# A perceiver block on one core: where the second quad's stacks stand, the first chunk in slices, a bias negated later and ternary weights stored in halves

## The reference

```
q = split_heads(layernorm(x) @ Wq, 16) * 32 ** -0.5
k = split_heads(ctx @ Wk, 16);  v = split_heads(ctx @ Wv, 16)
logits = einsum('bhqd,bhkd->bhqk', q, k) + bias          # bias 128 x 2048, the same for all heads
x = x + merge_heads(softmax(logits) @ v) @ Wo
ws = 1.0 / clip(mean(abs(w)), 1e-5)                      # for each matrix w_i, w_f, w_g, w_o, w_gate, w_down
wq = clip(round(w * ws), -1, 1) / ws                     # the ternary weights
```

## Time and profile before

| | before |
|---|---|
| median of 3 runs | 1146.83 us |
| profiled execution | 1147.05 us, span 1145.3 us |
| attention (0 to 710 us) | TensorE busy 660.66 us |
| the rest (710 to 1145 us) | TensorE busy 353.41 us |
| whole span | TensorE 1014.1 us (89%), VectorE 578.0 (50%), ScalarE 429.7 (38%), GpSimd 237.4 (21%) |

### The profile page before, as it was taken

The page is one execution under the profiler, slowest core; times in us unless marked ns, Lnnn a source line. Parts: engine busy times, 40 slices in busy tenths (PEclk is TensorE's granted clock), DMA queues, the critical chain, the costliest instruction groups (busy, mean ns, idle before and its releaser), DMA issues.

```text
span 1145.3 us, 17470 instructions
## 1 busy us (share of the span) xinstructions
PE 1014.1 (89%) x7046; PEld 791.6 (69%) x7046; DVE 578.0 (50%) x1180; ACT 429.7 (38%) x552; POOL 237.4 (21%) x201
## 2 busy tenths in 40 slices
PE   5799899999899997899999998426659999999997
PEld 4478677888677885677887674223347999977774
DVE  4433886456894644794448873786752111111110
ACT  1111676152783182784234771545611011111110
POOL 0300560002630002620003900543111011110000
PEclk9899999999999998999999999667767999999999
DMA  7063781515754217554125818000018997699910
GB/s 267 27 112 81 166 197 43 187 37 150 156 142 169 112 37 210 127 138 137 44 97 119 175 35 346 17 0 1 1 45 306 389 374 274 214 359 313 296 19 12
DMA packets 77753, 169.85 MB, mean 148 GB/s; under 512 B 7416, under 2 KB 17656, under 8 KB 72800
## 3 DMA queue, kind: packets, MB, share of 16 engines
q1 hardware_dynamic: 75552, 163.84, 46.9%
q0 software_dynamic: 2112, 4.80, 1.9%
HBM read 118.97 MB, written 16.10 MB: 118 GB/s over the span
## 4 chain that ended last, share of the span: by engine, by line
PE 77%; DVE 9%; issue 4%; DMA 3%; ACT 3%; POOL 3%; SPq 0%; DVEq 0%; POOLq 0%; ACTq 0%
PE psum L1590 10%; PE psum L451 8%; PE psum L431 6%; PE psum L1620 6%; PE psum L466 6%; PE psum L1605 5%; PE psum L370 5%; PE psum L387 5%; PE psum L371 5%; PE psum L388 4%; PE psum L389 4%; PE psum L372 4%; PE psum L419 1%; DMA stack<-stack 1%; PE psum L492 1%
## 5 line engine op out<-in xcount | busy, mean ns | idle before, releaser
L849 POOL CAST stack<-kT 128x2048 fp32r<-128x2048 f32 x40 | 77.5, 1963 | 444.4 <-ACT kT L732 403.2
L603 DVE CUSTOM_DVE_ANT_0 prob<-psum,biasmap,top 128x512 f32<-128x512 f32 x192 | 144.2, 751 | 25.6 <-PE psum L431 17.2
L451 PE MATMUL psum<-ident,prob 128*128 128x128 f32 x1024 | 136.2, 276 | 5.9 <-ACT probT L778 3.9
L770 ACT ACTIVATE prob<-prob,top 128x2048 f32<-128x2048 f32 x64 | 128.6, 2009 | 24.2 <-DVE top L603 24.2
L451 PEld LDWEIGHTS psum<-ident,prob 128*128 128x128 f32 x1024 | 118.4, 142 | 24.6 <-issue 10.8
L1590 PE MATMUL psum<-xT,wring 128*128 128x128 f32 (+3 forms) x1024 | 133.5, 291 | 0.6 <-ACT xT L1878 0.6
L1590 PEld LDWEIGHTS psum<-xT,wring 128*128 128x128 f32 x1024 | 131.4, 193 | 2.8 <-issue 1.9
L778 ACT COPY probT<-psum 128x1024 f32<-128x1024 f32 x96 | 96.5, 1010 | 57.8 <-PE psum L466 56.5
L732 ACT COPY kT<-psum 128x512 f32<-128x512 f32 x64 | 37.5, 586 | 206.2 <-PE psum L372 206.2
L370 PE MATMUL psum<-ctx_part,wk_hi 128*128 128x512 f32 x256 | 101.7, 397 | 13.6 <-DVE ctx_part L541 13.6
L1801 DVE TENSOR_SCALAR hidden<-psum,b 128x128 f32<-128x128 f32 (+3 forms) x64 | 23.6, 369 | 161.9 <-PE psum L1590 161.9
(11 more groups left out here) (231 smaller groups left out, 1471.0 us busy)
## 6 DMA issues: line engine op xcount, KB each, us to landing
wring<-in_w SPq DMA_DIRECT2D x64, 1024.0 KB, 9.9
ctx_raw<-in_ctx_t SPq DMA_DIRECT2D x16, 1024.0 KB, 6.2
stack<-stack SPq DMA_DIRECT2D x40, 256.0 KB, 4.9
stack<-key_stack SPq DMA_DIRECT2D x28, 256.0 KB, 4.5
ternary<-ternary_weights SPq DMA_DIRECT2D x1, 6272.0 KB, 24.6
prob<-in_w_gate_t SPq DMA_DIRECT2D x1, 5632.0 KB, 17.2
query_stacks<-prob SPq DMA_DIRECT2D x16, 256.0 KB, 5.4
qstack<-query_stacks SPq DMA_DIRECT2D x16, 256.0 KB, 5.5
```

What stands on the lines that cost most here:

```text
L451: mm = pe.transpose(psum[:, w + i, j * P:(j + 1) * P], prob[:, prob_slot(n, j), kt * P:(kt + 1) * P], ident[:, :])
L603: dve.tensor_tensor_reduce(prob[:, slot, keys], psum[:, scores.of[n, j, c], :], biasmap[:, keys], 1.0, top[:, h, (c + 1) % 2:(c + 1) % 2 + ...
L770: act.activation(prob[:, slot, :], prob[:, slot, :], ACT.Exp, bias=top[:, h, 1:2], scale=-1.0, accum_out=top[:, h, 2:3]).then_inc(*raised. ...
```

## The change

There are five edits.

- **Stacks.** Heads 1 to 3 of the second quad leave the ring. Their stacks stand in the four slots of `prob` in which the first quad had its stacks, which are the slots that the second quad's own scores go to: head j's cast waits until head j of the first quad has been scored. Head 0 of the second quad keeps a place of the ring (turn 0), and the third and fourth quads have turns 1 to 8.
- **Fillers.** The 16 row blocks are spread as 2, 1, 2, 1, ... over ten slots, where they were 2, 2, 1, ... over nine.
- **Ternary weights.** The mean is taken one tile earlier, and the store is two DMAs of half the pieces, each issued when its half is ready. What waited for the store waits for the second half.
- **First chunk.** Wk and chunk 0 come in four pairs of DMAs, one pair for each row block k of 128 rows (256 KB each). ScalarE casts the two slices of a block, VectorE subtracts, and TensorE does the 12 matmuls of that block for all four key tiles before the next block.
- **Bias.** GpSimd waits for the last of the four normalised rows of x before it negates the bias.

```diff
-FILLERS = (2, 2, 1, 2, 2, 1, 2, 2, 2)
+FILLERS = (2, 1, 2, 1, 2, 1, 2, 1, 2, 2)
...
-        self.mean_at = self.sum_at + len(self.sums) + 3
+        self.mean_at = self.sum_at + len(self.sums) + 2
         self.round_at = self.mean_at + 1
-        self.store_at = self.round_at + len(self.pieces) + 1
+        self.stores = [(half, self.round_at + (half + 1) * len(self.pieces) // 2 + 1) for half in range(2)]
...
+        def in_ring(n, j):
+            return n % DT >= 2 or n % DT == 1 and j == 0
+
         def ring_turn(n, j):
-            return QUAD * (n % DT - 1) + j
+            return QUAD * (n % DT - 2) + j + 1 if n % DT >= 2 else 0
+
+        def head_of_turn(b, turn):
+            return (DT * b + 2 + (turn - 1) // QUAD, (turn - 1) % QUAD) if turn else (DT * b + 1, 0)
...
         def stack_place(n, j):
-            if n % DT == 0:
-                return early_stack[:, (QUAD * (n + 1) + j) % PS, :]
-            return RING_PLACES[ring_turn(n, j) % len(RING_PLACES)]
+            if in_ring(n, j):
+                return RING_PLACES[ring_turn(n, j) % len(RING_PLACES)]
+            return early_stack[:, (QUAD * (n - n % DT + 1) + j) % PS, :]
...
+            def project_first_keys():
+                banks = [work.take(("keys", 0, 0, m), keys_copied.at(0, 0, m))[0] for m in range(DT)]
+                for k in range(DT):
+                    pe.wait_ge(*slice_low.at(k, "ctx"))
+                    ch, cl = ctx_part[:, 0, 0, k, :], ctx_part[:, 0, 1, k, :]
+                    for m, w in enumerate(banks):
+                        wh, wl = wk_hi[:, k, m * P:(m + 1) * P], wk_lo[:, k, m * P:(m + 1) * P]
+                        pe.matmul(psum[:, w, :], wh, ch, start=(k == 0), stop=False)
+                        pe.matmul(psum[:, w, :], wh, cl, start=False, stop=False)
+                        mm = pe.matmul(psum[:, w, :], wl, ch, start=False, stop=(k == DT - 1))
+                        if k == DT - 1:
+                            mm.then_inc(*keys_projected.made(0, 0, m))
+
+            project_first_keys()
...
                         project_value_tile(b, VTILES * c + i)
-                    elif b == 0 or (c, i) > (0, 0):
+                    elif c > 0 or b > 0 and i > 0:
...
+                    dve.wait_ge(*ternary_stored.at(b, 1))
+                elif (g, j, c) == (1, 0, 0):
...
-            dve.wait_ge(*wk_in.at("all"))
-            split(wk_hi[:, :, :], wk_lo[:, :, :], wk_sb).then_inc(*parts_split.made("wk"))
-            split_chunk(0)
+            for k in range(DT):
+                dve.wait_ge(*slice_high.at(k, "wk"))
+                dve.tensor_tensor(wk_lo[:, k, :], wk_sb[:, k, :], wk_hi[:, k, :].bitcast(F32),
+                                  ALU.subtract).then_inc(*slice_low.made(k, "wk"))
+                dve.wait_ge(*slice_high.at(k, "ctx"))
+                dve.tensor_tensor(ctx_part[:, 0, 1, k, :], ctx_raw[:, k, :], ctx_part[:, 0, 0, k, :].bitcast(F32),
+                                  ALU.subtract).then_inc(*slice_low.made(k, "ctx"))
             dve.wait_ge(*wv_in.at("all"))
             split(wv_hi[:, :, :], wv_lo[:, :, :], wv_sb).then_inc(*parts_split.made("wv"))
...
+            for k in range(DT):
+                act.wait_ge(*slice_in[k].at("ctx"))
+                act.copy(wk_hi[:, k, :], wk_sb[:, k, :]).then_inc(*slice_high.made(k, "wk"))
+                act.copy(ctx_part[:, 0, 0, k, :], ctx_raw[:, k, :]).then_inc(*slice_high.made(k, "ctx"))
...
+            pool.wait_ge(*row_normed.at(0, B - 1))
             pool.wait_ge(*bias_in.at("all"))
             pool.tensor_scalar(biasmap[:, :], biasmap[:, :], -1.0, None, ALU.mult).then_inc(*bias_negated.made("all"))
...
                 pool.wait_ge(*keys_copied.at(b, CHUNKS - 1, g))
                 for j in range(QUAD):
                     turn = ring_turn(n, j)
-                    if turn == 0:
+                    if not in_ring(n, j):
+                        pool.wait_ge(*scored.at(n - 1, j, UNITS - 1))
+                    elif turn == 0:
                         pool.wait_ge(*values_projected.at(b, VTILES * (CHUNKS - 1) - 1))
-                    if turn == 2:
+                    elif turn == 2:
                         pool.wait_ge(*keys_projected.at(b, CHUNKS - 1, DT - 1))
-                    if turn == 4:
+                    elif turn == 4:
                         pool.wait_ge(*keys_high(DT * b + 1, QUAD - 1))
-                    if turn >= len(RING_PLACES):
-                        before = turn - len(RING_PLACES)
-                        pool.wait_ge(*scored.at(DT * b + 1 + before // QUAD, before % QUAD, UNITS - 1))
+                    elif turn >= len(RING_PLACES):
+                        before = head_of_turn(b, turn - len(RING_PLACES))
+                        pool.wait_ge(*scored.at(*before, UNITS - 1))
                     pool.tensor_copy(stack_place(n, j), kT[:, g, :]).then_inc(*keys_high_g.made(n, j))
                     if j == 0:
                         if g == 1:
@@ -857,7 +890,7 @@
                         pool.tensor_tensor(LOW_PLACES[g % 2], kT[:, g, :], stack_place(n, 0).bitcast(F32),
                                            ALU.subtract).then_inc(*keys_low_g.made(n))
...
-                if tile == window.store_at:
-                    count, size = len(window.pieces), window.size
-                    lo = FIRST[window.mats[0]]
-                    sp.wait_ge(*made_ternary.at(b, count - 1))
-                    sp.dma_start(ternary_dram[:, lo:lo + count * size].rearrange("p (n s) -> p n s", n=count),
-                                 prob_flat[:, 0:count * size].rearrange("p (n s) -> p n s", n=count).bitcast(BF16)
-                                 [:, :, 0:size]).then_inc(*ternary_stored.made(b))
-
-            sp.dma_start(wk_sb, rows(a["wk"])).then_inc(*wk_in.made("all"))
-            load_ctx(0)
+                for half, store_at in window.stores:
+                    if tile == store_at:
+                        count, size = len(window.pieces) // 2, window.size
+                        first = half * count
+                        lo = FIRST[window.mats[0]] + first * size
+                        sp.wait_ge(*made_ternary.at(b, first + count - 1))
+                        sp.dma_start(ternary_dram[:, lo:lo + count * size].rearrange("p (n s) -> p n s", n=count),
+                                     prob_flat[:, first * size:(first + count) * size].rearrange(
+                                         "p (n s) -> p n s", n=count).bitcast(BF16)[:, :, 0:size]).then_inc(
+                                             *ternary_stored.made(b, half))
+
+            for k in range(DT):
+                sp.dma_start(wk_sb[:, k, :], a["wk"][k * P:(k + 1) * P, :]).then_inc(*slice_in[k].made("wk"))
+                sp.dma_start(ctx_raw[:, k, :], a["ctx_t"][0, k * P:(k + 1) * P, 0:CHUNK]).then_inc(
+                    *slice_in[k].made("ctx"))
             sp.dma_start(wv_sb, rows(a["wv"])).then_inc(*wv_in.made("all"))
             sp.dma_start(wq_sb, rows(a["wq"])).then_inc(*wq_in.made("all"))
             sp.dma_start(x_in, a["x"].rearrange("b s d -> s b d")).then_inc(*x_loaded.made("first"))
             sp.dma_start(biasmap[:, :], a["bias"]).then_inc(*bias_in.made("all"))
-            sp.wait_ge(*ctx_split.at(0))
+            sp.wait_ge(*slice_low.at(DT - 1, "ctx"))
             load_ctx(1)
```

36 lines of the change are left out of this document (18 added, 18 removed).

## The result

| | before | changed |
|---|---|---|
| median | 1146.78 us (4 runs) | 1115.23 us (4 runs, 1113.68 to 1117.76) |
| ratio | | 0.9727, 95% interval 0.9706 to 0.9747 |
| profiled execution | 1147.05 us, span 1145.3 | 1113.68 us, span 1111.9 |

The changed kernel is 31.6 us faster; forecast were 34.3 (1112.7). The profiled execution is the fastest of the first four runs, so what is read from it shows the kernel at its better end.

The account below looks back on a forecast made before the run. TensorE, the busiest engine, was taken as the bound, so only its idle time and slow clock counted. 13.9 + 10.8 + 1.4 + 3.0 + 5.2 = 34.3 us off 1147.05 gives 1112.7; 1108 to 1117 at 64%, wider range 1105 to 1122.

Parts of the forecast that it names:

- Start of TensorE at 7.0: First chunk: with the slices, TensorE's first matmul comes at about 7.0 us instead of 13.6.
- Chunk 1 still lands at 22.46, since the same bytes stand ahead of it: Front loads: chunk 1's landing stays at 22.46 us, and the query projection starts at 35.3 instead of 46.53.
- slices are slow: Rival, first loads: eight slices at half rate, 10.6 us instead of 5.3, chunk 1 5.3 us later, total 1118; 8%.
- The estimate from the Trainium skill's page: First chunk's loads: at 138 GB/s, 2.1 MB would take 15 us instead of 5, total near 1122.
- Fourth normalisation at 0.5 us: VectorE on x: without GpSimd's bias work on it, this instruction takes about 0.5 us instead of 5.61.
- Clock up in the projection, +2.7: Query projection: if the clock stays up, 2.7 us more are saved, making the front's gain 13.9 instead of 11.2.
- 2.7 us in each batch: Second quad's stacks and fillers: each batch wins 2.7 us, 10.8 for four; clock in batches 0 and 3 adds 3.0.
- Batch 2's 1.4 for the third quad's head 0: Batch 2: TensorE's 1.4 us wait for that head goes, as its stack is ready at 24 and needed at about 27.
- The store half: VectorE 5.3 us sooner, a wait of about 3 us: Batch 2's ternary weights: second half lands at 435.4 instead of 440.7, gain 5.2 us, TensorE still waits about 3.
- After the attention nothing, some 2 us either way: Stages after the attention: same work, no gain; clock changes there may shift the time some 2 us either way.
- VectorE becomes the bound: Rival, second stage: removed waits return as score-bank waits, batches win 1 us each instead of 2.7, total 1121; 12%.
- The reused places cost more: Rival, second quad: stacks landing later than 12 us stall three heads per batch; 1161 at 16 us of landing; 3%.

Follow-up runs that it names:

- e1_bias_first: Changed kernel with the bias negation back in its old place, before the fourth normalisation of x: 1123.32 us, 0.9791 of the kernel before.
- e7_bias_load_behind: Changed kernel with the bias loaded behind chunk 1 instead of ahead of it: 1114.65 us, 0.9698 of the kernel before.
- e4_store_whole: Changed kernel with ternary weights stored in one transfer per matrix group and the mean one tile later, as before: 1121.28 us, 0.9780 of the kernel before.
- e6_cast_behind: Changed kernel with GpSimd's first cast for the second quad also waiting for VectorE's cast of the first quad's head 1: 1114.5 us, 0.9703 of the kernel before.
- e10_again: Changed kernel run again unaltered, giving its second profile: 1118.49 us, 0.9738 of the kernel before.
- e5_old_fillers: Changed kernel with only the old filler spread (2,2,1,2,2,1,2,2,2), stacks in their new places: 1118.96 us, 0.9742 of the kernel before.
- e3_old_stacks: Changed kernel with the second quad's stacks back in the ring and the old fillers: 1132.2 us, 0.9876 of the kernel before.

## Why the prediction was right, and where its sizes were off

The mechanisms were those of the change: of the 34.3 us forecast, 31.6 came in the medians. Taken back one at a time, the bias, the first chunk, the stacks with the fillers and the two edits to the ternary weights cost some 7, 4.5, 16.5 and 5.5 us, 33.5 in all. The fillers by themselves can't be told from nothing by the time. By its steps:

- **Start of TensorE at 7.0.** It was 6.56, and 6.2 to 7.4 in the other profiles with eight slices. Right.
- **"Chunk 1 still lands at 22.46, since the same bytes stand ahead of it."** This step failed. It landed at 24.00 (23.7 to 24.7 in the seven profiles with the same queue): the bytes were the same, their rate was not. The rival "slices are slow" priced half the rate for all eight at 5.3 us; 1.5 us came. The estimate from the Trainium skill's page "DMA: Bandwidth & Descriptors" (§ Bandwidth) took its 138 GB/s, measured there for transfers of 64 KB issued from GpSimd, and that was too low for transfers of 256 KB queued one behind the other on SyncE: the slices moved at 175 to 284. Its direction was right. The projection started at 36.94 for 35.3, which is this 1.5 us.
- **Fourth normalisation at 0.5 us.** 0.55; undoing the edit brought 5.61 back (e1_bias_first). Right. No wait for the bias appeared. What the text did not price is the order of the loads: 1 MB of bias stands ahead of chunk 1, and moving it is worth 3.5 us (e7_bias_load_behind).
- **Clock up in the projection, +2.7.** Right in the first profile, 1.5 us short in the second, and 5.4 to 6.5 us for the first quarter in five of the others. It should have been half a gain: that the forecast took the whole of it and the first profile agreed was luck. In six profiles with the same front the first score came at 105.9 to 109.9, where 104.2 or 106.9 were forecast, a spread of 4 us, not 2.7. This is a good part of the 4 us over which the kernel's first four runs spread.
- **2.7 us in each batch.** The stalls went, and with them the clock's 1.5 in batches 0 and 3 (4.1 and 3.9 for 4.2). The 1.5 us of clock are read from one execution before and one after. The margin of a reused place was not "nearly 6 us", for its 4.3 us of landing were read where the queue was nearly idle: in batch 1 head 1's cast starts at 269.98, its last DMA is issued at 272.60 and lands some 6.5 us later, 1.9 us ahead of its score at 281.00. The step that failed is batch 1's, 0.8 for 2.7 in the first profile and 1.7 in the second: nothing in the text counted how full the DMA engines are in the first quad (0.95 of the time before, 1.00 now; over the two quads their share rose from 0.72 to 0.91), nor that a cast of GpSimd could fall on VectorE's small copy.
- **Batch 2's 1.4 for the third quad's head 0.** Gone, as forecast.
- **The store half: VectorE 5.3 us sooner, a wait of about 3 us.** VectorE was 5.2 us sooner than with the old store (e4_store_whole). The wait was 4.96, for the sum took VectorE's cast at its old 1.23 us, and at its new place it met GpSimd's (1.73 us; e6_cast_behind gives exactly those back). The gain of 3.3 is below the bounds of 3.7 to 6.5. The text had named this danger in its last sentence and priced it nowhere.
- **After the attention nothing, some 2 us either way.** It was 3.9 in the profile, 0.3 with the second profile of the same kernel. No edit of the change touches this stretch, so the 3.9 count among the 33.4 us of the profiles by luck. The granted clock does differ there (0.57 against 0.50 in the second 20 us behind the output projection's start), but that it makes the whole difference was not shown.

"VectorE becomes the bound" (12%) was wrong as a whole; batch 1 has waits for VectorE where GpSimd holds up its copy. "The reused places cost more" (3%) did not come, with less margin than thought.

Still open: why batch 1's transfers are slower than batch 3's, and what decides whether the clock falls around x. Where TensorE stood 2.2 to 3.4 us in one piece before the transposes of x (the profiles of e4_store_whole, e5_old_fillers and e6_cast_behind), the granted clock was 0.50 already in the transposes. With pieces of 1.5 us and less it fell in one (e10_again) and stayed at 1.00 in two (the base's first and e3_old_stacks).

## What to carry to other kernels

When a step is moved sooner, list what each other engine does at the new time, the engines that share a port and the DMA queue above all: the store's 5.2 us arrived whole, and 1.7 of them were lost to a cast that nobody needed yet. Order the loads by when they are needed, not only the work: putting 1 MB behind another brought some 3.5 us, where the rewrite of the first chunk brought some 4.5, each known to some 3 us. And price a wait of the busiest engine with the clock behind it: here the slot behind a wait of 4.6 to 5.0 us took 3.3 to 3.6 us, and behind one of 1.0 us 1.9. Before reusing a place, read the time to landing where the new transfers will run, not where the queue is idle.

## What the runs showed of the hardware

- Loads from memory queued back to back, mean of 3 to 7.5 us: 234 to 274 GB/s with 256 KB (eleven profiles), 330 with 512 KB, 374 and 375 with 1 MB (two profiles).
- Stretches in which the queue held mostly SBUF to SBUF transfers of 32 rows (9 of 11, the other two loads of queries): all 16 engines full at 216 to 223 GB/s. An estimate from it: a head's two of 256 KB take 2.4 us.
- VectorE beside a GpSimd cast that began first: cast of 2048 columns 2.96 us for 1.23, copy of 128 columns 1.83 for 0.23, tensor_scalar of 512 columns 5.61 for 0.55 (beside a 5.38 us one).
- Granted clock: a wait of 4.6 to 5.0 us before batch 2's first score was followed by a lower clock (0.50 to 0.55, first slot 3.3 to 3.6 us for 1.9) in each of the eight profiles that had it, one of 3.2 us in one of two (0.56 and 1.00), one of 1.0 us in none of two (1.00).
